# Cross-partition bounds by products with ones, and the Fourier loads issued from SP

## The reference, cut to what matters

```python
# x: 8 x 2048 x 512;  D_MODEL 512, D_STATE 16
xn    = layernorm(x) * ln_gamma + ln_beta
delta = sigmoid(xn @ w_delta + b_delta)        # 512 -> 16
B_t   = xn @ w_in + b_in                       # 512 -> 16
gate  = sigmoid(xn @ w_gate + b_gate)          # 512 -> 512
h_t   = tanh(h_(t-1) * delta_t @ A + B_t)      # scan over 2048 steps, 16 states
y     = (h @ C) * gate
x     = layernorm(x + y + x)
f     = real(ifft(fft(x) @ (w_freq_real + i w_freq_imag))) + bias
out   = layernorm(x + f)
```

## Time and profile before

| | us |
|---|---|
| median of 3 runs | 982.52 |
| lowest and highest | 982.04, 982.98 |
| span of the profiled execution, first to last instruction | 980.0 |
| TensorE busy | 929.7 (95%) |
| VectorE busy | 755.7 (77%) |
| ScalarE busy | 561.1 (57%) |
| GpSimd busy | 518.4 (53%) |

### The profile page before, as it was taken

The page is one execution under the profiler, slowest core; times in us unless marked ns, Lnnn a source line. Parts: engine busy times, 40 slices in busy tenths (PEclk is TensorE's granted clock), DMA queues, the critical chain, the costliest instruction groups (busy, mean ns, idle before and its releaser), DMA issues.

```text
span 980.0 us, 19706 instructions
## 1 busy us (share of the span) xinstructions
PE 929.7 (95%) x5742; PEld 516.0 (53%) x5742; DVE 755.7 (77%) x1616; ACT 561.1 (57%) x1047; POOL 518.4 (53%) x1317
## 2 busy tenths in 40 slices
PE   5899999999999999996998999999999999999996
PEld 2455555555555555553776555545545455454543
DVE  5598878888788787875668788787787877878774
ACT  2243333333333333343465588878888888888887
POOL 0152222222222222216114888889888898888984
PEclk9889999999999999997999999999999999999999
DMA  9144445554445554441603467676666676666753
GB/s 322 44 147 147 144 164 171 171 164 137 154 144 171 171 171 153 145 151 40 241 2 82 165 226 240 227 232 239 227 228 230 227 244 220 232 233 224 247 172 129
DMA packets 89483, 175.84 MB, mean 179 GB/s; under 512 B 3057, under 2 KB 5361, under 8 KB 89458
## 3 DMA queue, kind: packets, MB, share of 16 engines
q1 hardware_dynamic: 85856, 170.80, 51.9%
q10 hardware_dynamic: 3602, 4.74, 1.5%
HBM read 106.45 MB, written 67.11 MB: 177 GB/s over the span
## 4 chain that ended last, share of the span: by engine, by line
PE 47%; POOL 33%; issue 11%; DVE 4%; ACT 2%; ACTq 1%; DMA 1%; POOLq 1%; DVEq 0%
POOL x_sb L689 12%; PE bank L1164 11%; PE bank L1165 11%; PE bank L1167 11%; POOL rstd L635 7%; PE bank L1154 6%; POOL rnorm L713 4%; POOL scaled_mean L696 2%; POOL veps L633 2%; PE bank L1209 2%; POOL lift_bias L699 1%; PE bank L1188 1%; POOL rstd L715 1%; POOL nbias L717 1%; ACTq L437 1%
## 5 line engine op out<-in xcount | busy, mean ns | idle before, releaser
L926 DVE SCALAR_TENSOR_TENSOR lo_sb<-bank,hi_sb 128x512 f16<-128x512 f32 x256 | 176.7, 690 | 93.8 <-ACT hi_sb L444 73.0
L444 ACT ACTIVATE hi_sb<-bank 128x512 f16<-128x512 f32 x128 | 76.4, 597 | 291.4 <-PE bank L1154 280.6
L633 POOL TENSOR_TENSOR veps<-mv,c_eps 128x1 f32<-128x1 f32 x256 | 49.4, 193 | 311.3 <-DVE mv L907 296.3
L1164 PE MATMUL bank<-z_sb,hi_sb 128*128 128x512 f16 x512 | 194.2, 379 | 9.1 <-DVE w_ring L1098 7.9
L1164 PE MATMUL bank<-wg_hi,hi_sb 128*128 128x512 f16 x512 | 197.7, 386 | 4.6 <-DVE wg_lo L794 3.8
L1165 PE MATMUL bank<-wg_lo,hi_sb 128*128 128x512 f16 x512 | 197.8, 386 | 0.0
L1165 PE MATMUL bank<-z_sb,hi_sb 128*128 128x512 f16 x512 | 194.2, 379 | 0.0
L1154 PE MATMUL bank<-cst,norm_sb 128*128 128x128 f32 x1024 | 160.6, 280 | 24.8 <-DVE norm_sb L920 23.0
L689 POOL TENSOR_TENSOR x_sb<-x_sb,gate_sb 128x512 f32<-128x512 f32 x128 | 163.4, 1277 | 11.8 <-DVE gate_sb L1086 11.3
L635 POOL TENSOR_TENSOR rstd<-veps,c_half 128x1 f32<-128x1 f32 x256 | 139.8, 546 | 20.1
L1154 PEld LDWEIGHTS bank<-cst,norm_sb 128*128 128x128 f32 x1024 | 119.2, 142 | 51.1 <-DVE norm_sb L920 15.0
(11 more groups left out here) (157 smaller groups left out, 1220.5 us busy)
## 6 DMA issues: line engine op xcount, KB each, us to landing
x_sb<-x SPq DMA_DIRECT2D x63, 1024.0 KB, 6.2
gate_dram<-gate_sb SPq DMA_DIRECT2D x32, 1024.0 KB, 5.3
gate_sb<-gate_dram SPq DMA_DIRECT2D x32, 1024.0 KB, 5.3
out<-out_sb SPq DMA_DIRECT2D x31, 1024.0 KB, 5.3
h_rep<-fourier_constants ACTq DMA_DIRECT2D x2, 514.0 KB, 14.8
x_sb<-x SPq DMA_DIRECT2D x2, 512.0 KB, 6.5
w_ring<-w_gate SPq DMA_DIRECT2D x2, 512.0 KB, 6.3
w_re_sb<-w_freq_real ACTq DMA_DIRECT2D x1, 1024.0 KB, 11.5
```

Of the source, the lines that this page charges most:

```text
L926: nc.vector.scalar_tensor_tensor(lo_sb[:, k % 2].rearrange("p t r -> p (t r)"), ps_t[k % 2][:], ROW_SCALE, hi_sb[:, k % 2].rearrange("p t ...
L1164: nc.tensor.matmul(dst, hi_sb[:, k % 2, t], w_hi[:, t], start=(t == 0), stop=False)
```

## The change

The four reduces on GpSimd become three products with a matrix of ones on TensorE (`ones_sb`, 128x128 in f32): out[i, j] is then the sum over the partitions of column j, the same on every row i. For the three bounds that were maxima, the sum of 128 maxima takes the place of the maximum; it is an upper bound up to 128 times as large, so the halves are split at a coarser scale. The fourth was a sum already. The products go into TensorE's own order: the first between the two halves of `gate_bias_products`, the second in slot 3, the third, of two columns, in slot 121. VectorE reads the results from PSUM. The Fourier loads move from ScalarE's queue to SP's, behind the first octet's x tiles and ahead of the loop.

```diff
...
+        sum_of_maxima = (ps_z[0][:, 0:2], bank[7][:, 0:1])
+        w_sums_all = bank[7][:, 0:2]
...
@@ block.sync @@
             load_x(0, 1, s_xl)
+            for dst, src in WB_LOADS:
+                sp.dma_start(dst, src).then_inc(s_wb, 16)
...
@@ block.scalar @@
             act.dma_start(a_c_sb[:], a_and_c).then_inc(s_a_c, 16)
-            for dst, src in WB_LOADS:
-                act.dma_start(dst, src).then_inc(s_wb, 16)
...
@@ block.gpsimd @@
-                if isinstance(n, int) and n == -2:
-                    pool.wait_ge(s_amax, 1)
-                    pool.partition_all_reduce(amax_all[:, 0:2], amax[:, 0:2], P,
-                                              ABSMAX).then_inc(s_amax_all, 1)
-                if isinstance(n, int) and n == 2:
-                    pool.wait_ge(s_amax, 2)
-                    pool.partition_all_reduce(amax_all[:, 2:3], amax[:, 2:3], P,
-                                              ABSMAX).then_inc(s_amax_all, 1)
-                if isinstance(n, int) and n == TILES - 8:
-                    pool.wait_ge(s_w_abs_sum, 1)
-                    pool.partition_all_reduce(w_abs_all[:], w_abs_sum[:], P, SUM).then_inc(s_w_abs_all, 1)
-                    pool.partition_all_reduce(w_max_all[:], w_max[:], P, ABSMAX).then_inc(s_w_abs_all, 1)
...
@@ block.vector @@
                 dve.wait_ge(s_amax_all, 1)
-                wait_own(scales(0, 2))
+                wait_own(scales(0, 2, sum_of_maxima[0]))
...
                 dve.wait_ge(s_amax_all, 2)
-                wait_own(scales(2, 3))
+                wait_own(scales(2, 3, sum_of_maxima[1]))
...
                 dve.wait_ge(s_w_abs, 4)
-                nc.vector.tensor_reduce(w_max[:], w_abs[:], AX.X, ALU.max)
-                nc.vector.tensor_reduce(w_abs_sum[:], w_abs[:], AX.X, ALU.add).then_inc(s_w_abs_sum, 1)
+                nc.vector.tensor_reduce(w_sums[:, 1:2], w_abs[:], AX.X, ALU.max).then_inc(s_w_abs_sum, 1)
+                nc.vector.tensor_reduce(w_sums[:, 0:1], w_abs[:], AX.X, ALU.add).then_inc(s_w_abs_sum, 1)
...
@@ block.tensor @@
+            def sum_maxima(i):
+                pe.wait_ge(s_amax, i + 1)
+                src = (amax[:, 0:2], amax[:, 2:3])[i]
+                nc.tensor.matmul(sum_of_maxima[i], ones_sb[:], src, start=True,
+                                 stop=True).then_inc(s_amax_all, 1)
+
+            def sum_w():
+                pe.wait_ge(s_w_abs_sum, 2)
+                nc.tensor.matmul(w_sums_all, ones_sb[:], w_sums[:], start=True,
+                                 stop=True).then_inc(s_w_abs_all, 1)
...
                     if t % (KT // 2) == 0:
                         pe.wait_ge(s_wg[t // (KT // 2)], 16)
+                    if t == KT // 2:
+                        sum_maxima(0)
...
+                if isinstance(n, int) and n == 3:
+                    sum_maxima(1)
+                if isinstance(n, int) and n == TILES - 7:
+                    sum_w()
                 if exists(n):
                     products(n, k, v)
```

More of the change, by code:

```diff
@@ L31 @@
 AX = mybir.AxisListType
-ABSMAX = bass.bass_isa.ReduceOp.absmax
-SUM = bass.bass_isa.ReduceOp.add
 C_IDENT, C_BLOCKS = 0, P
@@ L109, in build @@
         w_abs = sb("w_abs", [P, 4])
-        w_abs_sum = sb("w_abs_sum", [P, 1])
-        w_abs_all = sb("w_abs_all", [P, 1])
+        w_sums = sb("w_sums", [P, 2])
         warm = sb("warm", [P, 1])
@@ L122, in build @@
         amax = sb("amax", [P, 3])
-        amax_all = sb("amax_all", [P, 4])
         amax_pos = sb("amax_pos", [P, 4])
@@ L160, in build @@
         m_hi, m_lo = halves_in(z_sb[:].rearrange("p (t n) -> p t n", t=KT))
-        w_max, w_max_all = sb("w_max", [P, 1]), sb("w_max_all", [P, 1])
+        w_max = sb("w_max", [P, 1])
         w_pow2 = sb("w_pow2", [P, 1])
@@ L188, in build @@
         ps_t, ps_g, ps_z, ps_x, ps_y = bank[0:2], bank[2:4], bank[4:6], bank[6], bank[6:8]
+        sum_of_maxima = (ps_z[0][:, 0:2], bank[7][:, 0:1])
+        w_sums_all = bank[7][:, 0:2]
+        m_bound = sb("m_bound", [P, 1])
         def c_share(i):
@@ L326, in build @@
         block = ctx.enter_context(nc.Block())
+        WB_LOADS = [
+            (w_re_sb[:], w_re.rearrange("(t p) n -> p t n", p=P)),
+            (w_im_sb[:], w_im.rearrange("(t p) n -> p t n", p=P)),
+            (cos_sb, dft[0].rearrange("(t p) n -> p t n", p=P)),
+            (sin_sb, dft[1].rearrange("(t p) n -> p t n", p=P)),
+            (cos_halves[:], dft_halves[0].rearrange("(t p) h n -> p t h n", p=P)),
+            (sin_halves[:], dft_halves[1].rearrange("(t p) h n -> p t h n", p=P)),
+        ]
         @block.sync
@@ L411, in _ @@
             sp.wait_ge(s_last, 16 * 4)
[L414 to L421, removed]
         @block.scalar
@@ L747, in largest, with scales @@
                                                apply_absolute_value=True)
-            def scales(a, b):
-                wait_own(nc.vector.tensor_scalar(amax_pos[:, a:b], amax_all[:, a:b], 1e-30, None, ALU.max))
+            def scales(a, b, bound):
+                wait_own(nc.vector.tensor_scalar(amax_pos[:, a:b], bound, 1e-30, None, ALU.max))
                 wait_own(nc.vector.tensor_scalar(pow2[:, a:b].bitcast(I32), amax_pos[:, a:b].bitcast(I32),
@@ L862, in sum_weights @@
                 dve.wait_ge(s_w_abs, 4)
-                nc.vector.tensor_reduce(w_max[:], w_abs[:], AX.X, ALU.max)
-                nc.vector.tensor_reduce(w_abs_sum[:], w_abs[:], AX.X, ALU.add).then_inc(s_w_abs_sum, 1)
+                nc.vector.tensor_reduce(w_sums[:, 1:2], w_abs[:], AX.X, ALU.max).then_inc(s_w_abs_sum, 1)
+                nc.vector.tensor_reduce(w_sums[:, 0:1], w_abs[:], AX.X, ALU.add).then_inc(s_w_abs_sum, 1)
             def scale_of_w():
-                dve.wait_ge(s_w_abs_all, 2)
-                wait_own(nc.vector.tensor_scalar(w_max[:], w_max_all[:], 1e-30, None, ALU.max))
+                dve.wait_ge(s_w_abs_all, 1)
+                wait_own(nc.vector.tensor_scalar(w_max[:], w_sums_all[:, 1:2], 1e-30, None, ALU.max))
                 wait_own(nc.vector.tensor_scalar(w_pow2[:].bitcast(I32), w_max[:].bitcast(I32), 0x7F800000,
@@ L879, in scale_of_m @@
             def scale_of_m():
-                wait_own(nc.vector.scalar_tensor_tensor(amax_all[:, 3:4], w_abs_all[:], 2.0 / D, bias_max[:],
+                wait_own(nc.vector.scalar_tensor_tensor(m_bound[:], w_sums_all[:, 0:1], 2.0 / D, bias_max[:],
                                                         ALU.mult, ALU.add))
-                wait_own(scales(3, 4))
+                wait_own(scales(3, 4, m_bound[:]))
             def scale_of_p():
```

## The result

The changed kernel takes **954.7 us**, the median of four executions (954.45 to 954.82); four executions of the kernel before take 982.28 (981.23 to 982.98). The ratio is 0.9722, with a 95% interval of 0.9708 to 0.9736. The change is worth 27.6 us, where the prediction had 24.1: 958.4, with a lowest time of 956.0. The profiled execution took 954.58, its span 952.8: 27.2 shorter than the span before.

A forecast was written before the change was run, and what follows sets the result against it. TensorE was taken to bound the kernel; 12.9 (start and second stop) + 11.5 (last stop) - 0.3 (small costs) = 24.1 off the 980.0 span leaves 955.9, plus 2.5 gives 958.4 us. The range was 956.0 to 961.8.

The forecast's parts named there:

- TensorE as the bound: Middle of the first pass: TensorE busy 80.00 of 80 us, so a microsecond off its path is one off the kernel.
- the three stops and their common cause: First pass: TensorE waits 3.82, 6.06 and 8.77 us, all behind GpSimd standing still around its reduces.
- the start with two causes that only fall together: Tile 0: first reduce and ScalarE's Fourier-load issue end within half a microsecond; together removed, scale chain starts 4.8 earlier.
- no third round of the scan: Scan: rival that coarser splitting changes a state and forces another round, giving 992; chance 0.03.
- no wait for Fourier loads: Fourier loads on SP land about 24 again, first used after 34; moving them costs nothing.
- normalise of tile 6: VectorE, first pass: forecast at 35.7 where it stood at 49.87, 14.2 earlier, before the clock term.
- The last stop: End of first pass, 440.14 to 458.43 on TensorE: 11.5 given back, bounds 11.4 and 11.7.
- VectorE did not become the bound: Behind tile 6 or at the pass's end: rival that VectorE gives 2 to 3 us back, 960.4 to 961.8; chance 0.15.
- the clock term: After the one-column products near the start: TensorE's clock falls again, costing 1.3, between nothing and 2.4.
- bound of 14.2: Start and second stop together: upper bound of their gain, 12.9 expected, lower bound 11.8.
- products with ones: TensorE: 0.3 us of its time each; only the third's 0.3 was subtracted in the sum.
- median less span: Whole kernel: median 982.52 lies 2.5 above the profiled span of 980.0, added to 955.9 to give 958.4.

The follow-up runs named there:

- thirteen executions: All profiled executions of the kernel before, the changed kernel and the follow-up variants; scan start to second-pass product took 69.77 to 69.89 in five with a clock fall, 68.61 to 68.73 in eight without.
- changed_look3: The changed kernel itself, unedited, profiled in a third execution to look at its clock; 955.66 us.
- changed_look2: The changed kernel itself, unedited, profiled in a second execution to look at its clock; 956.82 us.
- loads_late_scalar2: The changed kernel with the Fourier loads back on ScalarE, issued behind its high halves of tile 0 and the gate weights; 954.89 us.

## Why the prediction was wrong in size

**What held.** TensorE as the bound; the three stops and their common cause; the start with two causes that only fall together; no third round of the scan; no wait for Fourier loads. The places came out close: scale chain at 12.91 (12.8 forecast), first products at 16.80 (16.85), transposes of tile 2 at 22.55 (23.0), normalise of tile 6 at 35.24 (35.7). The last stop gave 26.3 - 14.8 = 11.5, as forecast. VectorE did not become the bound: it is busy 29.05 of 32 us from 412 to 444 while TensorE is busy all 32.

**The step that failed: the clock term.** "I expect a fall again ... I take the middle, 1.3" made 12.9 out of 14.2 (the middle of nothing and 2.4 is 1.2). In the profiled execution there is no fall. Nor does it stand alone where there is a fall: it was put on top of a start read from an execution in which the clock rose late, and in the changed kernel's executions that fell, the clock had risen early. The size of 1.3 for the fall itself was right (1.3 lost from tile 1 to tile 6, three times), but the earlier rise brings back 0.8 to 1.5. In the executions seen the right term was 0, within 0.5, and the bound of 14.2 on the gain was the better value. The clock term alone doesn't explain the miss: without it the sum gives 957.1, still inside the range. The other lines below all err to the same side, and the sum had no room for that.

**The account of the miss.** 958.4 less 954.7 is 3.7:

| | us |
|---|---|
| clock term that did not come | 1.3 |
| path to the normalise of tile 6, 14.6 instead of 14.2 (the other bias products took 2.86 us, 19.69 to 22.55, not 3.35) | 0.4 |
| from there to 51.73, where TensorE no longer ran slowly behind the stop | 0.3 |
| products with ones: 0.15, not 0.3 | 0.15 |
| start of the second pass 1.1, of which 0.2 is lost again | 0.9 |
| median less span: 2.5 assumed, 1.9 found | 0.6 |

The fifth line was not in the sum at all. In the trace of before, the clock falls at the start of the second pass, and the first profile after has none there:

```profile
536.00:540.00 4.00, 2.16 (x11) 1.34 (x11) 3.93 (x8) 2.35 (x4) 3.69 (x8) 0.91 0.59 139
540.00:542.00 2.00, 1.91 (x6) 0.61 (x6) 1.96 (x4) 1.30 (x2) 1.84 (x4) 0.50 0.99 383
542.00:544.00 2.00, 2.00 (x9) 0.87 (x8) 1.59 (x4) 0.00 (x0) 1.84 (x5) 0.83 0.15 55
```

By the thirteen executions above, this 1.1 belongs to the executions that happened to be profiled and not to the change: that it fell to the changed kernel's side is luck. changed_look3, with the fall, took 955.66, still 0.3 below the range; changed_look2 took 956.82, inside it, but with the 1.3 of the second pass. The mean granted clock of an execution tells which kind it is: 0.998 in the first profile, 0.994 in these two. The four timed executions read 0.998, 0.995, 0.998 and 0.998, so at least three of them had no more falls than the first profile.

The sixth line is a matter of reading. Each execution's time is 1.8 us above its own span, in every run here (954.58 and 952.8; 964.04 and 962.2). The prediction took median less span, 2.5, of which 0.7 is how much quicker the profiled execution of before was than its median.

## What to carry to other kernels

Look at what an engine stands still around, not at how long an instruction lasts: two reduces of 0.4 us cost 11.6 us of TensorE, and three products of 0.15 replace them all. When two waits end at nearly the same time, cost the edits together and once each alone, since the sum of the singles says nothing. And before putting a fall of the clock into a sum, look whether it is in more than one execution, and whether a late or early rise came with it; a single trace has one draw of both.

## What was not expected of the hardware

The pause on GpSimd behind a `partition_all_reduce`, before ordinary work runs again, was 6.79 to 8.64 us in all fifteen places of the seven profiles that have reduces, longer than the one ahead of it (5.59 to 6.17 in ten places; 8.21 to 8.75 ahead of the first reduce, which also waits for its maxima). It comes back whenever a reduce does. It is paid once for a group: of two reduces in a row, the second starts with no pause (426.05 and 426.37 above).

The time for which an issue held its engine differed tenfold: up to 4.62 us on SP in the changed kernel, where the DMA share was 1.05, against 0.39 for the first of the same loads in loads_late_scalar2 at 13.92, where the share was 0.26 from 12 to 14. It isn't the share alone: the last of the six took 1.38 on SP, at a share of 1.05 too. The cause was not tried by itself. SP and its queue in the changed kernel:

```profile
3.89 0.58 SPq L359 DMA_DIRECT2D w_re_sb<-w_freq_real  x1
...
10.80 4.62 SPq L359 DMA_DIRECT2D cos_halves<-fourier_halves  x1
15.47 1.38 SPq L359 DMA_DIRECT2D sin_halves<-fourier_halves  x1
23.47 0.39 SPq L341 DMA_DIRECT2D x_sb<-x  x1
```

TensorE's clock took different courses in executions of one and the same program: at the start it reached its full rate early or late, worth up to 1.5 us at tile 1, and fell afterwards or not. The Trainium skill, "TensorE: Matmul & The Clock Gate", section "Part 1: The HAM clock gate (the "warmup" mystery)", says that one kernel measures different numbers of slow products from run to run; the starts here agree. At the start the profile's granted clock reads 1.00 from 8 us on even where the lengths of the products (0.42 against 0.28) show half rate: there the lengths are the ones to read.
